# Selective scan: the odd unit's two tiles in one scan instruction of 1024 columns

## The reference, cut to what matters

```
dt = jax.nn.softplus(dt + dt_proj_b)
A = -jnp.exp(A_log)
deltaA = jnp.exp(dt[..., None] * A)
deltaB_u = dt[..., None] * Bm[:, :, None, :] * x[..., None]
_, states = jax.lax.associative_scan(_scan_op, (deltaA, deltaB_u), axis=1)
y = jnp.sum(states * Cm[:, :, None, :], axis=-1) + x * D
```

## Time and profile before

| | |
|---|---|
| time of three runs | 2966.15, 2975.92, 2981.10 us (median 2975.92) |
| the profiled execution's own time | 2962.07 us |
| its span, first to last instruction | 2959.9 us |
| PE busy | 2566.8 us, 87% |
| DVE busy | 1955.7 us, 66% |
| POOL busy | 1369.1 us, 46% |
| ACT busy | 1254.2 us, 42% |

### The profile page before, as it was taken

How to read it: one execution, slowest core, us unless ns; L and a number is a source line. 1 busy time by engine, 2 the same in 40 slices (tenths; PEclk the granted TensorE clock), 3 DMA queues, 4 the chain that set the end, 5 groups by cost and what they waited for, 6 DMA issues and landing times.

```text
span 2959.9 us, 33617 instructions
## 1 busy us (share of the span) xinstructions
PE 2566.8 (87%) x11874; PEld 1513.4 (51%) x11938; DVE 1955.7 (66%) x2271; ACT 1254.2 (42%) x2016; POOL 1369.1 (46%) x719
## 2 busy tenths in 40 slices
PE   6998848888898999998748889978988879999998
PEld 2444624444577999865213233333333323577776
DVE  4667865554455666565379899889989887742223
ACT  3433114431123656433445655564555443243333
POOL 0222236650040000051079999999999888122221
PEclk9999769999899999999879999999999889999999
DMA  6443963322063767541135555545545555300000
GB/s 211 132 139 96 96 115 82 75 89 90 11 225 117 249 233 250 183 163 52 58 92 168 147 148 162 164 141 159 174 151 145 145 168 159 132 1 15 11 5 29
DMA packets 277527, 368.47 MB, mean 124 GB/s; under 512 B 126816, under 2 KB 148320, under 8 KB 272256
## 3 DMA queue, kind: packets, MB, share of 16 engines
q1 hardware_dynamic: 271680, 341.28, 39.6%
q0 software_dynamic: 5120, 16.78, 1.6%
q10 hardware_dynamic: 576, 8.39, 0.7%
HBM read 314.74 MB, written 63.18 MB: 128 GB/s over the span
## 4 chain that ended last, share of the span: by engine, by line
PE 60%; DVE 20%; issue 7%; POOL 5%; ACT 4%; DMA 2%; SPq 1%; DVEq 0%; PEldq 0%; POOLq 0%; PEld 0%; ACTq 0%
PE psum L1848 7%; PE psum L1983 4%; PE psum L1984 4%; PE psum L1797 4%; DVE psum L1399 3%; POOL arena L738 3%; DVE arena L1399 3%; PE psum L2600 2%; PE psum L2787 2%; POOL arena L744 2%; DVE arena L1404 2%; PE psum L1696 2%; PE psum L1698 2%; PE psum L1697 2%; PE psum L1887 2%
## 5 line engine op out<-in xcount | busy, mean ns | idle before, releaser
L738 POOL TENSOR_TENSOR arena<-arena 128x1024 f32<-128x1024 f32 x256 | 640.0, 2509 | 174.2 <-DVE arena L1389 111.1
L1848 PE MATMUL psum<-arena,cst 128*128 128x512 f32 x1024 | 517.0, 643 | 183.5 <-POOL arena L744 114.9
L974 ACT ACTIVATE psum<-arena,negA 128x512 f32<-128x512 f32 x512 | 333.4, 682 | 319.7 <-DVE arena L1399 278.6
L1848 PEld LDWEIGHTS psum<-arena,cst 128*128 128x128 f32 x1024 | 193.8, 200 | 491.2 <-issue 199.9
L1399 DVE TENSOR_TENSOR_SCAN arena<-psum,arena 128x512 f32<-128x512 f32 x256 | 310.6, 1213 | 70.9 <-ACT psum L974 54.9
L744 POOL TENSOR_TENSOR arena<-arena 128x1024 f32<-128x1024 f32 x128 | 311.5, 2434 | 21.2 <-DVE arena L1399 21.2
L1399 DVE TENSOR_TENSOR_SCAN psum<-psum,arena 128x512 f32<-128x512 f32 x256 | 297.7, 1208 | 32.4 <-POOL arena L738 32.4
L765 POOL TENSOR_TENSOR arena<-arena 128x512 f32<-128x512 f32 x64 | 94.3, 1474 | 332.5 <-ACT arena L1086 301.1
L1797 PE MATMUL psum<-arena 128*128 128x512 f32 x512 | 231.2, 595 | 1.3 <-PE psum L1797 0.8
L711 POOL DMA_INDIRECT arena<-o_scr,r_ix x32 | 33.5, 1046 | 380.7 <-DMA o_scr<-arena 371.5
L2146 POOL TENSOR_TENSOR arena<-arena,cst 128x512 f32<-128x512 f32 x64 | 77.5, 1238 | 279.3 <-DVE arena L2446 192.8
(11 more groups left out here) (330 smaller groups left out, 5182.4 us busy)
## 6 DMA issues: line engine op xcount, KB each, us to landing
arena<-bc_scr SPq DMA_DIRECT2D x256, 512.0 KB, 5.0
arena<-w_exp SPq DMA_DIRECT2D x23, 1408.0 KB, 6.1
arena<-in_gu SPq DMA_DIRECT2D x48, 512.0 KB, 4.9
arena<-in_inw SPq DMA_DIRECT2D x32, 512.0 KB, 4.0
arena<-in_dn SPq DMA_DIRECT2D x31, 512.0 KB, 6.9
x_scr<-arena SPq DMA_DIRECT2D x23, 512.0 KB, 6.8
arena<-x_scr SPq DMA_DIRECT2D x23, 512.0 KB, 7.2
o_scr<-arena SPq DMA_DIRECT2D x23, 512.0 KB, 5.7
```

What stands on the lines that cost most here:

```text
L738: nc.gpsimd.tensor_tensor(dB[:, k % 4], du[:, j:j + 2], BC[:, k % RING, 0].unsqueeze(1).broadcast_to([P, 2, T]), ALU.mult).then_inc(s["db_ ...
L974: nc.scalar.activation(psum[:, bank], dt[:, b % 2, j + t], ACT.Exp, scale=negA2[:, at:at + 1]).then_inc(s["da_ok"], 1)
L1848: ins = mm(psum[:, t], ident, dB[:, k % 4, t], start=False, stop=(n == NS - 1), skip_group_check=True)
```

## The change

An odd unit's two tiles are scanned by one instruction over 1024 columns, banks 2 and 3 read as one row. So that nothing of the first tile's last state enters the second tile, the decay of every tile's first column is made zero: after `times_dt` has made du, a memset sets dt's first column of the half's four tiles to 1e25, and exp(1e25 * A) is 0. The scan waits for both decays of its unit and counts both tiles at its end. The decays wait for du_ok, which the memset raises, where they waited for sp_f. The even unit is scanned as before.

```
+DT_END = 1e25
...
                 if i % 32 == 0 and t == 0:
-                    act.wait_ge(s["sp_f"], 2 * b + i // 32 + 1)
+                    act.wait_ge(s["du_ok"], 2 * b + i // 32 + 1)
...
             def times_dt(b, h):
                 dve.wait_ge(s["sp_f"], 2 * b + h + 1)
                 dve.wait_ge(s["c_sil"], NDT * b + 4 * h + 4)
-                v.tensor_tensor(du[:, 4 * h:4 * h + 4], dt[:, b % 2, 4 * h:4 * h + 4], xs[:, b % 2, 4 * h:4 * h + 4],
-                                ALU.mult).then_inc(s["du_ok"], 1)
+                ch.link(v.tensor_tensor(du[:, 4 * h:4 * h + 4], dt[:, b % 2, 4 * h:4 * h + 4], xs[:, b % 2, 4 * h:4 * h + 4],
+                                        ALU.mult))
+                v.memset(dt[:, b % 2, 4 * h:4 * h + 4, 0], DT_END).then_inc(s["du_ok"], 1)
...
                 dve.wait_ge(s["da_ok"], 2 * k + t + 1)
-                dA = psum[:, 2 + t if k % 2 else 6]
-                h = dA if k % 2 else dB[:, k % 4, t]
-                v.tensor_tensor_scan(h, dA, dB[:, k % 4, t], 0.0, ALU.mult, ALU.add).then_inc(s["sc"], 1)
+                v.tensor_tensor_scan(dB[:, k % 4, t], psum[:, 6], dB[:, k % 4, t], 0.0, ALU.mult, ALU.add).then_inc(s["sc"], 1)
+
+            def scan_both(k):
+
+                dve.wait_ge(s["db_ok"], k + 1)
+                dve.wait_ge(s["da_ok"], 2 * k + 2)
+                dA = psum[:, 2:4].rearrange("p a t -> p (a t)")
+                v.tensor_tensor_scan(dA, dA, dB[:, k % 4].rearrange("p a t -> p (a t)"), 0.0, ALU.mult, ALU.add).then_inc(s["sc"], 2)
...
                     scan(k, 1)
-                    scan(k + 1, 0)
-                    scan(k + 1, 1)
+                    scan_both(k + 1)
```

## The result

Six runs of the changed kernel have a median of 2990.18 us (2987.41 to 2995.91), six of the kernel before 2974.88. The ratio is 1.0049, 95% interval 1.0027 to 1.0072. So the change makes the kernel slower, by half a per cent: about 15 us by the first ratio, 17 by the second, where +10 was forecast.

What follows compares the result with a forecast made beforehand. POOL and DVE were both taken as near their limit in the scan stage. Terms of 7.0, 0.2, 1.0 and 2.0 us gave +10.2 us on the 2975.9 us median: 2986 us, range 2973 to 2999.

Steps and rivals of the forecast that it cites:

- tight pairs: Pairs of units where DVE runs all five instructions without a gap; 58 of 128, each growing 0.26 us to 5.87.
- the border of 0.5%: Forecast's limit for telling a change from none: 15 us, so slower begins at 2991 us.
- The chance of 0.27 for slower: Forecast's probability that the whole kernel gets slower by over 0.5%; within 0.5% had 0.70.
- The hand-over: From the end of ACT's decay to the start of DVE's waiting scan: 0.03 us.
- the saving: DVE time saved by each merged scan: 0.06 us, bounds 0 and 0.14.
- the 27 pairs on the chain: Tight pairs whose odd scans lie on the stage's chain of waits: 27 x 0.26 = 7.0 us.
- the pair paced by ACT: Pairs whose even scan waits for ACT's decay: 37, +0.02 us each, a third on the chain, 0.2 us.
- the 90 forecast: Pairs in which the merged scan should wait for ACT's decay: some 90, 20 us or more in all.
- The rival in which every tight pair counts: Delays in all 58 tight pairs reach POOL's second product: 18 us, or 23 with nothing saved; chance 0.22.
- the pairs off the chain: The 31 tight pairs beside the chain of waits: 8.1 us held, a quarter let through, 2.0 us.
- The memsets: Eight on DVE, about 0.22 us each with link, 1.8 us in all, 1.0 us of it on the path.
- the first scan waits for POOL: Pairs whose first odd scan waits for POOL's product: 33, nothing added and zero gained.

Runs made afterwards that it cites:

- E2: The kernel before, with only the odd unit's first scan waiting for both decays; two scans, no memset: ratio 1.0039, stage 1020.7 us.
- E1: The changed kernel timed again, unaltered: ratio to the kernel before 1.0058, stage 1027.2 us.
- E4: The changed kernel with the merged scan raising its semaphore by one instead of two, wait numbers adapted: ratio to before 1.0033, stage 1019.1 us.
- E9: E4 with the merged scan's two waits in the other order, the decays' wait named first: ratio to before 1.0032, stage 1013.7 us.
- E7: E4 with DVE's other work of a pair moved ahead of the merged scan: ratio to before 0.9996, stage 1005.0 us.
- E6: The kernel before plus one memset of four unused columns and its link, once, ahead of the first scan: ratio 1.0003, stage 1010.2 us.
- E3: The kernel before plus the memset, its link and the decays' wait for du_ok, scans as before: ratio 1.0034, stage 1011.9 us.

## Why the prediction was right, and where its sum was short

*The direction and the mechanism held.* The forecast was a small loss, from a merged scan that must wait for ACT's second odd decay in 58 tight pairs. The waits view counts 57, and E2 shows that this wait without the merge costs most of the loss. The measured 2990 us lies in the range, and +0.49% is just inside the border of 0.5% that the forecast drew; E1's +0.58% is just outside. The chance of 0.27 for slower may have been too low: the two ratios put the price at 0.5 to 0.6%, on the border itself. That the time came out so near the forecast is in part luck: two terms below were too small, and the single profiles differ by more than the ratio, 18.4 us in the stage and 1.8 behind it.

*The tight pair was mis-sized: 0.40 us for 0.26.* Two terms are at fault. The hand-over was taken as 0.03 us from a scan with a single wait. The merged scan has two waits and an increment by two, so both waits stand in an instruction of their own, and it starts 0.13 us behind the decay. E4 and E9 bring that to 0.10 and to 0.03 or 0.04. The other 0.04 is the saving, taken as 0.06 us from a product of two sizes; the scan's own is 0.02 (2.21 for 2.23 us to the next instruction). The trace of before held no scan of 1024 columns. E2 shows that neither the merge nor the increment is needed for most of the first error: there the scan comes 0.10 us behind the decay as well. In E7's pair with a convolution, where the merged scan follows another instruction than a scan, the saving is 0.05. With 0.40, the 27 pairs on the chain come to 10.8 us, for 7.0.

*So was the pair paced by ACT: 0.15 us for 0.02.* There the odd scan started 1.14 us behind the second even scan and now starts 1.32 us behind it, and in E9, with the short hand-over, 1.22, which is what the prediction had. Twelve of these 37 pairs are on the chain, before and after, as forecast; they come to 1.8 us and not 0.2. Their wait is too short for the waits view, which counts 57 pairs and not the 90 forecast; the 20.8 us in all are as forecast. With both corrections the prediction's sum is 10.8 + 1.8 + 1.0 + 31 x 0.40 / 4 = 16.7 us.

The Trainium skill ("Perfetto Trace Analysis", Optimizing Scalar/DVE Operations) gives about 125 ns per instruction for access to PSUM on DVE. That is further off than the 0.06 us: the measured saving is 0.02 to 0.05 us. The same section says that breaking instructions up may let work be completed sooner where DVE isn't saturated but makes others wait. This case agrees: in 57 pairs the first of the two scans could start where the merged one must wait, and POOL's waits for PE grew from 62.5 to 84.8 us.

*The chain's count of 27 fits, but the totals don't prove it.* In the chain of the changed kernel 22 of the 57 waiting scans lie on it, and 21 of 56 in E1; 22 x 0.40 is 8.8 of the stage's 18.4 us. Batches 1 to 3, where the kernel before repeats to 0.1 us, hold 19 of these pairs. They grew from 255.1 + 253.2 + 258.3 = 766.6 us to 261.4 + 257.1 + 257.2 = 775.7: +9.1, where 19 x 0.40 gives 7.6. That leaves 1.5 us for all other pairs, but so small a rest can't be read: the same three batches take 770.4 us with E6's nudge, 762.5 in E3 and 777.0 in E4. The rival in which every tight pair counts asks for 58 x 0.40 = 23 us at the measured price, over the stage's 18.4, of which half is batch 0 alone; at its own price of 18 us the total would not have excluded it. What the pairs off the chain let through stays open.

*Batch 0 was not foreseen.* It grew from 240.5 or 244.0 us to 251.4, +7 to +11, with eight of the 27 pairs in it (3.2 us). The excess goes with a lower granted clock of PE at the stage's start, 0.87 for 0.90 to 0.92, where sums of eight matmuls take 5.2 to 6.6 us in place of 3.7. How many of the microseconds the clock makes is not shown. The prediction did not look at the clock.

*The memsets* took 0.06 us each and not 0.19; their link and the moved wait show no cost of their own in batches 1 to 3 of E3. The 1.8 us behind the stage, in every kernel that has them, were in no term.

*Confirmed:* the first scan waits for POOL in 35 pairs (33 before), and these gained nothing: the merged scan starts 0.09 us behind the product, for 0.03, and the next instruction comes 2.21 us after it, for 2.25. A pair waiting for ACT with its even scan did so 37 times, as before.

## What to carry to other kernels

Before joining two instructions of one engine, look at when the second one's input is ready: the join moves its wait ahead of the first, and here 0.34 us of idle time in 54 of 57 places stood against 0.02 us saved in each. Where work that depends on nothing late stands behind such a wait, move it in front; that alone made this kernel faster by 0.2%. In this kernel the wait named first sat in the scan itself, and an increment by one kept it there; naming the late one first saved 0.07 us at each such wait, though the kernel's time did not show it.

## What the runs showed of the hardware that was not expected

- The time from a decay's end to the scan that waits for it was 0.03 us with the wait inside the scan (E9), 0.10 with that wait in an instruction of its own (E2, E4), and 0.13 with two waits there, which is what an increment by two led to. Swapping the two waits swapped the delays of the scans that wait for ACT and for POOL.
- A scan of 1024 columns takes 2.299 us and the next instruction starts 2.21 us after it; two of 512 take 2.32 and 2.23. Its cost is all but proportional to its columns, while a product has 0.06 us beside them.
- The stage's first batch is 240 to 251 us long at granted clocks of 0.93 to 0.87, and the same kernel can give 240.5 and 244.0. The other three batches repeat to 0.1 us in the kernel before, but one memset ahead of the stage made one of them 2.9 us longer.
- Every kernel with the eight memsets is 1.8 us longer behind the stage, where nothing was changed. The cause was not found.
